# Two score units in a row: how a hand-merged step list places its attention pairs

## The reference, cut to what matters

```python
xn = _layernorm(x)
x = x + _L0_attn_ref(xn, ...) + _L0_ffn_ref(xn, ...)

# _L0_attn_ref: per chunk of 16 tokens and head, local and atrous (step 3)
attn = softmax(einsum('bhqd,bhkd->bhqk', q, k) * SCALE); out = einsum('bhqk,bhkd->bhqd', attn, v)
return _linear(local_out + atrous_out, Wo, bo)

# _L0_ffn_ref: causal attention over all 512 tokens, then experts
scores = einsum('bqhd,bkhd->bhqk', qq, kk) * scale; scores = where(causal, scores, min)
probs = softmax(scores); y = einsum('bhqk,bkhd->bqhd', probs, v)
x = x + (y @ W_o)
x = x + moe(rmsnorm(x, w_ln2), ...)   # one shared and seven routed experts, two chosen per token
```

## Time and profile before

| | before |
|---|---|
| median of 3 runs | 393.47 us (393.38 to 396.17) |
| span of the profiled execution | 387.9 us |
| what lies around it, up to the median | 5.6 us |
| TensorE busy | 337.9 us (87%) |
| VectorE busy | 286.0 us (74%) |
| ScalarE busy | 224.1 us (58%) |
| GpSimd busy | 122.7 us (32%) |
| instructions | 11664 |

### The profile page before, as it was taken

How to read it: one execution, slowest core, us unless ns; L and a number is a source line. 1 busy time by engine, 2 the same in 40 slices (tenths; PEclk the granted TensorE clock), 3 DMA queues, 4 the chain that set the end, 5 groups by cost and what they waited for, 6 DMA issues and landing times.

```text
span 387.9 us, 11664 instructions
## 1 busy us (share of the span) xinstructions
PE 337.9 (87%) x4504; PEld 205.0 (53%) x4504; DVE 286.0 (74%) x720; ACT 224.1 (58%) x545; POOL 122.7 (32%) x148
## 2 busy tenths in 40 slices
PE   5678987898898988998688889878999999999994
PEld 4366654454465445464445455445445755665663
DVE  6987668798666898878679978879623569668644
ACT  4356434676576465664467658656665564746462
POOL 6286407210600472603301400000201365444543
PEclk9988998999999999999999999999999999999998
DMA  8453141333105033350211331206000000000100
GB/s 193 82 197 100 26 155 43 89 56 65 27 22 160 24 69 54 84 167 3 64 41 30 58 65 48 43 6 161 3 2 0 3 0 27 3 28 0 30 0 27
DMA packets 29141, 21.84 MB, mean 56 GB/s; under 512 B 12312, under 2 KB 26008, under 8 KB 29048
## 3 DMA queue, kind: packets, MB, share of 16 engines
q1 hardware_dynamic: 28872, 20.91, 21.9%
q10 hardware_dynamic: 216, 0.20, 0.2%
HBM read 6.81 MB, written 6.19 MB: 34 GB/s over the span
## 4 chain that ended last, share of the span: by engine, by line
PE 48%; DVE 28%; ACT 10%; issue 7%; SPq 3%; DMA 1%; ACTq 1%; POOL 1%; DVEq 0%; POOLq 0%
PE bank_B L1428 11%; DVE neg_max L1068 6%; PE bank_c L1332 6%; PE bank_A L1434 5%; PE bank_B L1236 5%; PE bank_A L1374 5%; ACT p_mla L886 3%; DVE s_loc L1085 2%; DVE row_max L1082 2%; ACT k_diag L830 2%; PE bank_M L1272 2%; SPq L624 1%; PE bank_M L1382 1%; DVE k_diag L1193 1%; PE bank_M L1397 1%
## 5 line engine op out<-in xcount | busy, mean ns | idle before, releaser
L886 ACT ACTIVATE p_mla<-bank_B 128x512 f32<-128x512 f32 (+1 forms) x176 | 94.3, 562 | 62.7 <-PE bank_B L1222 61.9
L1068 DVE TENSOR_REDUCE neg_max<-bank_A 128x1 f32<-128x512 f32 (+3 forms) x176 | 108.6, 637 | 19.5 <-PE bank_A L1222 15.8
L1236 PE MATMUL bank_B<-q_stack,k_stack 54*128 54x512 bf16 (+3 forms) x256 | 63.2, 303 | 10.9 <-DVE neg_max L1068 5.1
L1215 PE MATMUL bank_A<-k_stack,q_stack 52*128 52x512 bf16 (+3 forms) x256 | 63.7, 303 | 0.1
L1428 PE MATMUL bank_B<-xrT,k_diag 128*128 128x512 f32 x128 | 61.7, 600 | 1.2 <-DVE k_diag L1193 1.0
L759 POOL TENSOR_TENSOR x<-x,q_part 128x512 f32<-128x512 f32 x31 | 39.4, 1272 | 61.3 <-ACT q_part L920 43.0
L1332 PE MATMUL bank_c<-p_mla,v_mla 128*32 128x128 f32 (+12 forms) x512 | 47.5, 444 | 5.6 <-ACT p_mla L886 5.5
L1236 PEld LDWEIGHTS bank_B<-q_stack,k_stack 54*128 54x128 bf16 x256 | 19.2, 93 | 54.0 <-issue 23.1
L920 ACT ACTIVATE q_part<-bank_A,expert_w 128x128 f32<-128x128 f32 x108 | 30.8, 368 | 28.8 <-PE bank_A L1434 28.8
L1193 DVE SCALAR_TENSOR_TENSOR k_diag<-k_diag,bank_B 128x512 f32<-128x512 f32 x32 | 22.0, 687 | 31.5 <-ACT k_diag L904 30.3
L1222 PE MATMUL bank_A<-masks 64*128 64x64 bf16 (+2 forms) x352 | 43.1, 202 | 0.0
(11 more groups left out here) (150 smaller groups left out, 568.8 us busy)
## 6 DMA issues: line engine op xcount, KB each, us to landing
v_dram<-v_rows SPq DMA_DIRECT2D x12, 324.0 KB, 3.6
k_stack<-parts SPq DMA_DIRECT2D x48, 64.0 KB
q_stack<-parts SPq DMA_DIRECT2D x45, 64.0 KB
k_diag<-k_part SPq DMA_DIRECT2D x48, 34.0 KB
v_diag<-v_dram SPq DMA_DIRECT2D x32, 45.0 KB, 2.1
v_diag<-v_dram SPq DMA_DIRECT2D x32, 36.0 KB, 2.1
v_dram<-v_rows SPq DMA_DIRECT2D x4, 283.5 KB, 2.8
x<-in_x SPq DMA_DIRECT2D x4, 256.0 KB, 8.0
```

What stands on the lines that cost most here:

```text
L886: drained_by(nc.scalar.activation(p_of(n)[:, m:m + len(heads), 0:w], src, ACT.Exp, scale=SCALE), step)
L1068: drained_by(nc.vector.tensor_reduce(neg_max[:, g, m:m + len(heads), i], src, AX.X, ALU.max, negate=True), step)
L1215: return nc.tensor.matmul(bank_of(step)[:, n * w:(n + 1) * w], q_stack[b % 2][rows, h % 8, i * P:(i + 1) * P], k_stack[b % 2][rows, h % 8, ...
L1236: nc.tensor.matmul(bank_of(step)[:, m * w:(m + 1) * w], k_stack[b % 2][rows, h % 8, j * P:(j + 1) * P], q_stack[b % 2][rows, h % 8, j * P: ...
```

## The change: two pairs to an entry

`scores()` now makes one entry of `BLOCK = 2` pairs: both S and both E, and behind them the PV steps that are due and the SHIFT. An empty entry follows each full block, so that the number of entries, and with it the spacing, stays as it was. Each group of 11 is cut into five blocks of two and one pair alone. All other lists, `SPREAD`, the rings and buffers are untouched; no instruction is added or taken away.

```diff
+BLOCK = 2
...
-            for k in range(PER_GROUP):
-                unit = []
-                if here:
-                    unit.append(("S", here[0], PER_GROUP * GROUP_ORDER.index(here[1]) + k))
-                if back:
-                    unit.append(exps[k])
-                found.append(unit + late + (shift if k == 1 else []))
-                late = []
-                if back and (k + 1 == PER_GROUP or exps[k + 1][3] != exps[k][3]):
-                    late = [("PV",) + exps[k][1:4]]
-                if back and k == OUTPUT_AT and n > LEAD:
+            for k0 in range(0, PER_GROUP, BLOCK):
+                block, done_j = [], []
+                ks = range(k0, min(k0 + BLOCK, PER_GROUP))
+                for k in ks:
+                    if here:
+                        block.append(("S", here[0], PER_GROUP * GROUP_ORDER.index(here[1]) + k))
+                    if back:
+                        block.append(exps[k])
+                        if k + 1 == PER_GROUP or exps[k + 1][3] != exps[k][3]:
+                            done_j.append(("PV",) + exps[k][1:4])
+                found += [block + late + (shift if 1 in ks else [])] + [[]] * (len(ks) - 1)
+                late = done_j
+                if back and OUTPUT_AT in ks and n > LEAD:
```

## The result

The changed kernel takes 402.02 us (median of 4 runs, 399.03 to 403.21) against 393.43 us for the kernel before beside it (4 runs, 391.83 to 396.17): a ratio of 1.0247, interval 1.0188 to 1.0306. It is slower by 8.6 us, and outside the range of the forecast, 390 to 401 us. The profiled execution took 402.07 us for a span of 400.3 us, 12.4 us more than the span before. These 12.4 us overstate the loss: every timed run lies 1.7 to 1.8 us above its span, so the profiled execution of the kernel before, with 387.9 us, was about 3.8 us quicker than the median, while that of the changed kernel was a median one.

The account below looks back on a forecast made before the run. No single bound: TensorE's many short waits, and SyncE's DMA queue in three stretches (some 86 of 266 us). Terms sum to +2.7 us, less 0.7 for overlap, so +2 us: 389.9 + 5.6 = 395.5 us, range 390 to 401.

Parts of the forecast that it names:

- Maxima behind local scores: At LS(0,1), (0,2), (1,0), (1,2), (3,2) the second pair waits for s_loc: +4.0 us; LS(3,4) gains: -0.5 us.
- A reading that was off: TensorE's idle time: 20.4 us for VectorE's reduction, 6.6 us for local scores in ring A, 9.8 us for PV's exponentials.
- Rival 2: Bursts starve single-buffered local steps PT, LO, LT: +12 us, some 8 us left, 401 us; chance 0.25.
- Exits: Steps leaving paired units: 51 fewer, 31 outside queue-ruled stretches, about 0.10 us each: -3.1 us.
- The queue: SyncE's DMA queue: SHIFT(0,1) moves ahead of ST(1,0), delaying the exponential of (0,3): +2.0 us (bounds 0.9 and 2.4).
- the clock is no term: Granted clock read nine tenths of full speed in 36 of 40 slices, so no time was priced for it.
- The first local scores: S(0,7) goes ahead of them into their 0.94 us wait for k_diag: -0.8 us (bounds -0.9 and 0).
- PV: Goes one pair later for three of four key blocks, giving its exponential more time: -0.8 us (bounds 0 and -3).
- LR, PT, LO and LT: Local steps behind a block: two exponentials run before LR, +1.2 us; LT(3,4) waits for VectorE's division, +0.7 us.
- The time around the span: Median 393.47 us lies 5.6 us above the profiled span of 387.9 us; carried over to the forecast.

Follow-up runs that it names:

- e13: Changed kernel with three banks in ring A, two in ring B and SyncE's old queue order: 398.16 us, ratio 1.0138.
- A3 B2: Ring setting: three banks in ring A and two in ring B, before 2 and 3; changed order 401.21 us, old order 399.32 us.
- e1: Changed kernel with only SyncE's queue put back in the order of the kernel before: 400.32 us, ratio 1.0185.
- e4: Kernel before with only SyncE's queue in the changed kernel's order, no blocks: 399.77 us, ratio 1.0168.
- e12: Changed kernel with fourteen extra matmuls ahead of TensorE's wait for the shift of group (0,3): 402.92 us, ratio 1.0227.
- e5: Kernel before with blocks of two only in the two last groups of entries (the tail): 395.20 us, ratio 1.0132.
- e9: Changed kernel with three banks in ring A and two in ring B: 401.21 us, ratio 1.0170.
- e15: Changed kernel with four buffers for p_mla in place of two: 402.43 us, ratio 1.0260.
- e6: Kernel before with blocks of two only in the first six groups of entries: 400.53 us, ratio 1.0283.
- e2: Changed kernel with five blocks directly behind local scores (LS) taken apart: 400.92 us, ratio 1.0231.
- e3: Changed kernel with SyncE's old queue order and the five blocks behind local scores taken apart: 400.13 us, ratio 1.0191.
- e7: Kernel before with blocks of two only from the seventh group of entries on: 397.36 us, ratio 1.0212.
- e10: Kernel before with three banks in ring A and two in ring B: 399.32 us, ratio 1.0120.

## Why the prediction was wrong, point by point

**The step that failed** is "*Maxima behind local scores*". It priced ring A only where a second maxima unit follows LS, and took every other block as free on that ring. The LS waits came as written (the pair behind LS(1,0) waits 1.23 us, forecast 1.2; waits of maxima units for s_loc rose from 3.7 to 8.6 us), but taking those blocks apart brought back 2 us at equal clock, not 4, and the same ring cost more elsewhere: pairs waiting for neg_max +2.5 us, LS directly behind a block +2.8 us. All of ring A went from 10.1 to 20.2 us of idling. The swap of one bank, which takes that away in both orders, shrinks the distance from 8.6 to 1.9 us (7.9 to 0.5 at equal clock). So some 5 to 7 of the 8.6 us hang on ring A's two banks, where the forecast had +4.0 - 0.5. That accounts for 1.5 to 3.5 us of the 6.6 us by which the forecast fell short. The savings that did not show (the first local scores and PV, 1.6 us together) account for a part of the rest; the remainder is open.

**A reading that was off.** The prediction called 20.4, 6.6 and 9.8 us of the earlier trace rows TensorE's idle time. They are the idle time of its weight loads, which overlap matmuls; the matmuls waited 5.1, 3.7 and 5.5 us for the same three, of 31.3 us between 40 and 300 us.

**Rival 2** named the mechanism, bursts of two, but the wrong place: the single-buffered local steps. TensorE's idle in all else did grow by 5.4 us, just past the 5 us from which I said it would decide. But e13 has far more of it (27.1 against 15.4 us in its control) and is no slower, so I read that growth as time that other savings give, not as the cause; no run isolates it. The rival's time, 401 us, was near the result, and for the reason it gave that was luck.

**Exits** (31 x 0.10 us): no run isolates them. A rough check is TensorE's busy time, in which a lower clock and the exits both show. Half of the time at the lower level is what the clock can add at most. Changed against before, busy time changed by -0.2 us where the clock would give +3.7; with A3 B2 by -5.6 where it would give +1.4; with the old queue as well by -12.1 where it would give -5.6. What is left is a saving of 3.9, 7.0 and 6.5 us, around the 51 x 0.10 = 5.1 us that all the places would give, and above the 3.1 us of the 31 alone. If entries cost as much as exits, as the mode-switch rule of the Trainium skill in TensorEngine Tiling (Array Packing), Key Properties, would allow, it should be 10.2 us, and none of the three comes near it. This is argued from sums, not shown by an experiment, and saved busy time can turn into other waits.

**The queue** (+2.0): order and mechanism as forecast, SHIFT(0,1) ahead of ST(1,0), all 2 to 3 us late, E(0,3) late behind its DMA. The wait grew by 3.0 us, and undoing it brought 2 us at equal clock (e1). What the forecast lacked is the clock: "the clock is no term" was read from the kernel before, and a wait of 2.9 us made it one in e4, for 2.0 us in the stretch behind it. In the changed kernel itself that second price could not be got back (e12), and its four runs have the same mean clock, 0.975, as the kernel before (0.974), so there it is not shown to cost anything on the whole.

**The first local scores** (-0.8): nothing came. LS(0,0) started at 35.19 us, 0.75 later than before, with S(0,7) now in front and 0.29 us of waiting for neg_max behind it. The clock was already low there from 32.4 us on (34.2 us before), which is part of the 0.75; at the SHIFT of (0,0) +0.3 us is left.

**PV** (-0.8): its waits fell from 5.5 us to 0.2, more than forecast, and in the tail, where nothing else moved, the time fell by 0.5 us with 1.3 of doubt (e5).

**LR, PT, LO and LT** (+1.9): of the right sign (waits for pT_loc before LT 1.2 to 2.7 us); no run isolates their price.

**The time around the span** was taken as 5.6 us; in every timed run it is 1.7 to 1.8. The other 3.8 us are that the profiled execution before was a quick one. Carrying the 5.6 us over comes to adding the +2 us to the median, which is what a forecast of a median should do, so this misreading did no harm.

## What to carry to other kernels

Before grouping units of a kind, count the banks or buffers of each ring that they pass: a burst costs from the unit that exceeds what the ring has free (two banks shared with another user hold one unit, not two), at every place and not only beside the other user. As a first price take the consumer's time for one unit (0.64 us of neg_max here; the waits of pairs for it were 0.5 us on the mean with blocks of two and 0.7 with three), and look for what stands directly behind the burst as well as for what was inside it. And a wait of some 3 us on TensorE may not be priced by its length alone: ask what the clock does after it.

## What the runs showed of the hardware

- TensorE's wait for the shift's DMA and the clock, by profile: in waits of 4.77 us (e9), 4.08 (changed), 4.02 (e15), 3.73 (e6) and 3.58 us (e2) the clock fell before the wait was over and stayed at the lower level for some 3 to 7 us; of the waits of 2.6 to 2.9 us, that in e4 went the same way, in e3 the clock fell 0.8 us after the wait, and in e13 it did not fall; after 0.99 to 1.83 us (e7, before, e10, e1, e5) it stayed up.
- With blocks of three no wait for ring A was longer than 3.0 us, and yet the clock stood low for 88 us of the span: it fell with many short waits close together, and without one long one. Of the 61 us that these blocks cost, the clock's part lies between 19 and 38 us.
- The same kernel varies by 15 us from run to run (386.7 to 402.2 us for the kernel before over 50 runs, on four chips), and the granted clock (0.957 to 0.992 in these runs) goes with two thirds of that variance.
